# Cross-attention matrices of seven batches made in the first batch's walk, kept in DRAM and loaded per batch

## The reference, cut to what matters

```python
q = einsum('bqm,mhd->bqhd', layernorm(x), Wq) + bq      # bq is not zero here
k = einsum('bkm,mhd->bkhd', ctx, Wk) + bk
v = einsum('bkm,mhd->bkhd', ctx, Wv) + bv
attn = softmax(einsum('bqhd,bkhd->bhqk', q / sqrt(64), k))
x = x + einsum('bqhd,hdm->bqm', einsum('bhqk,bkhd->bqhd', attn, v), Wo) + bo
```

## Time and profile before

| | us |
|---|---|
| three runs | 1469.76, 1473.22 (median), 1481.17 |
| the profiled execution | 1470.44 |
| its span, first to last instruction | 1468.6 |
| PE busy | 1324.8 (90%) |
| DVE busy | 835.2 (57%) |
| POOL busy | 688.1 (47%) |
| ACT busy | 611.2 (42%) |

### The profile page before, as it was taken

How to read it: one execution, slowest core, us unless ns; L and a number is a source line. 1 busy time by engine, 2 the same in 40 slices (tenths; PEclk the granted TensorE clock), 3 DMA queues, 4 the chain that set the end, 5 groups by cost and what they waited for, 6 DMA issues and landing times.

```text
span 1468.6 us, 22253 instructions
## 1 busy us (share of the span) xinstructions
PE 1324.8 (90%) x6717; PEld 841.1 (57%) x6718; DVE 835.2 (57%) x2358; ACT 611.2 (42%) x1278; POOL 688.1 (47%) x1113
## 2 busy tenths in 40 slices
PE   6886899899989998998899889988989789999995
PEld 5542456556655665566556655665566246666663
DVE  2627654864595369436853775386548623333348
ACT  2231554155415531643265236424541544444456
POOL 4312353454445353635354545444544445555557
PEclk9998899999999999999999999999999899999998
DMA  6053204110501050105000500240032534422255
GB/s 215 1 164 127 84 1 122 52 31 1 144 30 31 1 155 19 30 8 162 20 15 29 144 17 15 65 108 17 1 108 66 157 111 129 129 86 86 86 201 175
DMA packets 78300, 115.38 MB, mean 79 GB/s; under 512 B 24840, under 2 KB 66208, under 8 KB 75648
## 3 DMA queue, kind: packets, MB, share of 16 engines
q1 hardware_dynamic: 67888, 79.69, 18.2%
q10 hardware_dynamic: 3840, 16.78, 4.3%
q0 software_dynamic: 6480, 17.77, 3.4%
HBM read 70.22 MB, written 43.59 MB: 77 GB/s over the span
## 4 chain that ended last, share of the span: by engine, by line
PE 59%; DVE 21%; ACT 7%; issue 4%; POOL 4%; ACTq 2%; DMA 2%; SPq 0%; POOLq 0%; DVEq 0%
PE ps L1097 9%; DVE ps L1559 8%; PE ps L930 7%; PE ps L911 6%; PE ps L1019 5%; PE ps L1006 4%; PE ps L1114 4%; PE ps L1061 4%; PE ps L980 3%; PE ps L945 2%; ACTq L1230 2%; PE ps L1071 2%; ACT room L1239 2%; PE ps L1041 2%; PE ps L881 2%
## 5 line engine op out<-in xcount | busy, mean ns | idle before, releaser
L1559 DVE CUSTOM_DVE_ANT_0 ps<-ps,mask_wide 128x128 f32<-128x128 f32 (+3 forms) x512 | 236.9, 522 | 43.6 <-PE ps L980 43.4
L1239 ACT ACTIVATE room<-ps 128x512 f32<-128x512 f32 x320 | 179.8, 599 | 151.4 <-PE ps L1006 151.1
L1061 PE MATMUL ps<-hT,w 128*128 128x512 f32 x768 | 204.5, 410 | 0.0
L706 POOL TENSOR_SCALAR_AFFINE_SELECT room<-room 128x256 f32<-128x256 f32 (+1 forms) x320 | 120.9, 388 | 136.9 <-ACT room L1239 132.2
L1061 PEld LDWEIGHTS ps<-hT,w 128*128 128x128 f32 x768 | 140.4, 188 | 31.4 <-DVE hT L1591 2.0
L980 PE MATMUL ps<-room 96*128 96x128 bf16 (+3 forms) x512 | 110.5, 311 | 51.9 <-DVE nm L1559 38.9
L1071 PE MATMUL ps<-w,room 128*128 128x256 f32 x512 | 132.4, 388 | 15.2 <-POOL room L758 15.0
L758 POOL TENSOR_TENSOR room<-room 128x512 f32<-128x512 f32 x64 | 85.5, 1336 | 117.1 <-DVE room L1603 85.9
L1097 PE MATMUL ps<-room 128*128 x284 | 135.4, 599 | 1.9 <-ACT room L1299 1.9
L930 PE MATMUL ps<-room 128*128 128x256 f32 x512 | 123.2, 385 | 2.8 <-ACT room L1200 1.8
L911 PE MATMUL ps<-room,xnT 128*128 128x512 f32 x256 | 122.0, 601 | 0.0
(11 more groups left out here) (234 smaller groups left out, 2370.1 us busy)
## 6 DMA issues: line engine op xcount, KB each, us to landing
room<-parts_d SPq DMA_DIRECT2D x48, 256.0 KB, 9.0
room<-parts_d ACTq DMA_DIRECT2D x48, 256.0 KB, 6.6
room<-xs_d SPq DMA_DIRECT2D x71, 129.0 KB, 2.1
parts_d<-room SPq DMA_DIRECT2D x64, 128.0 KB, 1.8
room<-pair_d SPq DMA_DIRECT2D x8, 1024.0 KB, 8.2
room<-in_L_ffn_ew SPq DMA_DIRECT2D x24, 256.0 KB, 5.3
xin<-in_x SPq DMA_DIRECT2D x8, 512.0 KB, 11.4
parts_d<-xnT SPq DMA_DIRECT2D x32, 128.0 KB, 1.8
```

What stands on the lines that cost most here:

```text
L706: done(g.affine_select(out=w, in_=w, compare_op=ALU.is_ge, fill=0.0, base=0, pattern=[[0, 2]] * (blocks - 1) + [[1, P]], channel_multiplie ...
L1061: last = mm(bank(up_banks(b, m)[i]), w[:, x, k, m * P:(m + 1) * P], hT[:, y, k, :], start=((x, y, k) == terms[0]), stop=((x, y, k) == term ...
L1239: done(fn(prob[:, u * 512:(u + 1) * 512], bank(score_bank(b) + n % 2), ACT.Exp), "b_exp")
L1559: last = v.tensor_tensor_reduce(bank(nmax % 2 * 2 + i, n), bank(nmax % 2 * 2 + i, n), mask_wide[:, S - n:S], 1.0, LOWEST, ALU.add, ALU.max ...
```

## The change

`m`, `bqk` and `vw` leave the step list of walks 1 to 7. In walk 0 they stay for batch 0, and the 16 `kv` steps become 48 `early` steps. For each pair of heads: `kv` (keys and values, two PSUM banks), `mh` twice (the two halves of M for batches 1 to 7), `bh` (bqk), `vh` twice (VW). In `mh`, `bh` and `vh` the two heads of a pair lie in partitions 0 to 63 and 64 to 127 and are multiplied as two row tiles of PE, each with a contraction of 64 and its own bank, with no block-diagonal zeros. ACT and DVE copy one bank each in the first 30 early steps, ACT both in the rest. ACT issues the stores: per pair one for M (7 batches x 128 x 1 KB), two for bqk, four for VW (64 x 4 x 1 KB each). The staging tiles lie in the room of w1 and w3.

Per batch SP now issues `load_m` (1 MB, and a 4 KB row spread to 128 partitions) once the previous walk's four `sc_add` are done, and `load_vw` (1 MB) ahead of `send_shifts(c, 1)`. `bq_bc` is no longer made per batch. `interleaved()` spreads the scores from `x_turn` 1 on, over 23 slots where there were 28 from `bqk` 0 on, so `sum` 0 and `x_bias` now stand ahead of score unit 7 of group 0, where they stood behind unit 11's (counting on into group 1). The list of walks 1 to 7 up to `ct` 0 becomes: x_turn 0, x_turn 1, sc 0, sc 1, shift 1, f_hb, cs 00, sc 2, sc 3, cs 01, sc 4, sc 5, sc 6, exp 0, sum 0, x_bias, cs 10, va 0 0, sc 7, cs 11, sc 8, sc 9, ct 00, va 0 1.

```diff
 PER = dict(
+    m_in=32, vw_in=16, m_ps=10, m_act=8, m_dve=2, ...
+ONCE = ("kv_in", "bq", "m_ps", "m_act", "m_dve")
+NOT_FIRST = ("y", "y_out", "m_in", "vw_in")
-CROSS = [
+CROSS_FIRST = [
...
+CROSS = [s for s in CROSS_FIRST if s[0] not in ("m", "bqk", "vw")]
-    first, last = CROSS.index(("bqk", 0)), CROSS.index(("ct", 3, 1))
+    first, last = CROSS.index(("x_turn", 1)), CROSS.index(("ct", 3, 1))
+EARLY = [("kv", 0), ("kv", 1)]
+for _a in range(PAIRS):
+    EARLY += [("mh", _a, 0), ("mh", _a, 1), ("bh", _a), ("vh", _a, 0), ("vh", _a, 1)] + ([("kv", _a + 2)] if _a + 2 < PAIRS else [])
+SHARED = 30
 def first_walk():
...
+        crossed += s[0] in ON_PE
+        at_max = s[0] == "max" and (s[1] * T + s[2]) % 3 != 2
+        count = {"v": 2, "route": 3, "slots": 4}.get(s[0], 1 if at_max or s[0] in ON_PE and crossed % 4 == 0 else 0)
+        order += [("early", i) for i in range(n, min(n + count, len(EARLY)))]
 # SP
+            def load_m(b):
+                done(sp.dma_start(m_in, m_d[b, :, :, :, :]), "m_in", 16)
+                done(sp.dma_start(bqk_in, bqk_d[b, :].partition_broadcast(P)), "m_in", 16)
+            def load_vw(b):
+                done(sp.dma_start(vw, vw_d[b, :, :, :]), "vw_in", 16)
                 if c is not None:
+                    if b is not None:
+                        before(sp, c, "y")
+                        load_vw(b)
                     send_shifts(c, 1)
-                        load_kv(b + 1)
+                        need(sp, b, "sc_add", T)
+                        load_m(b + 1)
                     if c is None:
-                        for i in range(4):
-                            sp.wait_ge(kv_out[i], 16 * 2 * PAIRS // 4)
+                        early_landed()
                         sp.sem_inc(freed, 1)
-                        load_kv(b + 1)
+                        load_m(b + 1)
 # PE
+                    if kind == "early":
+                        lo, hi = (4, 5) if n % 2 == 0 else (6, 7)
+                        if n >= 2:
+                            pe.wait_ge(pre["act"], n - 1)
+                            pe.wait_ge(pre["dve"], min(n - 1, SHARED))
...
+                            for c2 in range(2 if what == "vh" else 1):
+                                for i, to in enumerate((lo, hi)):
+                                    rows = slice(i * CHD, (i + 1) * CHD)
+                                    if what == "mh":
+                                        last = mm(bank(to, (B - 1) * CK), wqT[rows, a, k * P:(k + 1) * P], kT[a % 2][rows, CK:], ...)
+                                    elif what == "bh":
+                                        last = mm(bank(to, (B - 1) * CK)[0:1, :], bq[rows, a:a + 1], kT[a % 2][rows, CK:], ...)
+                                    else:
+                                        last = mm(bank(to, D, c2 * D), vT[a % 2][rows, at:at + P], wo_c[rows, a, :], ...)
                     elif kind == "x_turn":
+                        if c is not None and step[1] == 0:
+                            need(pe, c, "a_max", per["a_max"] - 1)
 # ACT
+            def store_early(n):
+                act.wait_ge(pre["act"], n + 1)
+                act.wait_ge(pre["dve"], min(n + 1, SHARED))
+                if what == "mh":
+                    act.dma_start(m_d[1:B, :, a, :, :].rearrange("b p k n -> p b (k n)"), m_st[a % 2]...)
...
+                    if kind == "early":
+                        act.wait_ge(pre["ps"], n + 1)
+                        if EARLY[n][-1] == 0 and what == "mh" and a >= 2:
+                            act.wait_ge(pre[f"m_out{a % 2}"], 16 * (a // 2))
+                        if what == "bh" and a >= 1:
+                            act.wait_ge(pre["bqk_out"], 16 * 2 * a)
+                        for i, src in enumerate((lo, hi)[0:1 if n < SHARED else 2]):
...
+                        if n:
+                            store_early(n - 1)
                     elif kind == "w_split":
+                        store_early(len(EARLY) - 1)
+                        (waits for every store)
 # DVE
                     elif kind == "cs" and step[2]:
+                        elif t == 0:
+                            need(dve, c, "m_in", 32)
+                            need(dve, c, "scat", per["scat"])
+                            if c == 0:
+                                dve.wait_ge(p0["split"], 2)
```

More of the change, by code:

```diff
@@ L145, in first_walk @@
         order.append(s)
[L146 to L151, removed]
+        crossed += s[0] in ON_PE
+        at_max = s[0] == "max" and (s[1] * T + s[2]) % 3 != 2
+        count = {"v": 2, "route": 3, "slots": 4}.get(s[0], 1 if at_max or s[0] in ON_PE and crossed % 4 == 0 else 0)
+        order += [("early", i) for i in range(n, min(n + count, len(EARLY)))]
+        n = min(n + count, len(EARLY))
+    assert n == len(EARLY), n
     return order + [("w_split",)]
@@ L240, in xattn_ffn @@
         wo = sb("wo", [P, KD, D])
+        with nc.sbuf_tensor("early", [P, 4 * KD * FF], F32) as early:
+            pass
         w1 = sb("w1", [P, 2, KD, FF], F32R)
@@ L338, in xattn_ffn @@
         av = sb("av", [P, 512])
+        bqk_st = [t.rearrange("p (b n) -> p b n", n=CK) for t in (early[0:1, 7680:7680 + (B - 1) * CK], av[0:1, 0:(B - 1) * CK])]
         st1 = sb("st1", [P, T, 6])
@@ L709, in batch @@
                         if c == 0:
-                            for i in range(2):
-                                pool.wait_ge(kv_out[i], 16 * 2 * PAIRS // 4)
+                            pool.wait_ge(pre["ps"], len(EARLY))
                         need(pool, c, "xn2", T)
@@ L876, in batch @@
                             need(pe, b, "kv_in", 64)
-                        if c is not None and half == 0:
-                            need(pe, c, "a_max", per["a_max"] - 1 + k)
                         for a in range(4):
@@ L910, in batch @@
                         for k in range(KD):
-                            last = mm(bank(half), xnT[:, k, t * P:(t + 1) * P], m_sb[:, k, half * 512:(half + 1) * 512], start=(k == 0), stop=(k == KD - 1))
+                            last = mm(bank(half), xnT[:, k, t * P:(t + 1) * P], m_sb[:, k, half * 512:(half + 1) * 512] if c is None else m_in[:, half * 4:half * 4 + 4, k, :], start=(k == 0), stop=(k == KD - 1))
                         if half:
@@ L1459, in batch @@
                         s3 = s_sb[:, t % 2, :].rearrange("p (h k) -> p h k", h=CH)
-                        done(v.tensor_tensor(s_sb[:, t % 2, :], ps[:, 0:1024], bqk, ALU.add), "sc_add")
+                        done(v.tensor_tensor(s_sb[:, t % 2, :], ps[:, 0:1024], bqk if c is None else bqk_in, ALU.add), "sc_add")
                         need(dve, b, "sc_add", t + 1)
```

204 lines of the change are left out of this document (130 added, 74 removed).

## The result

The changed kernel takes **1550.62 us** (1547.11 to 1552.59, four runs) where the kernel before takes 1472.46 on the same chip: a ratio of **1.051, interval [1.047, 1.056]**. The forecast was 1496, with 1525 as the end of its range. The direction was right, the size was not: +78 us where I had about +26.

What follows compares the result with a forecast made beforehand. PE looked full in the walks, but new waits of 7.8 us would offset 9.25 removed; DMA and hand-overs bound walk 0. Walk 0 and the step to walk 1 +38, six walks -12, on 1470.4: 1496, range 1452 to 1525.

Steps and rivals of the forecast that it cites:

- What waits instead: Walk 2: PE idles 2.8 us before `sc` 0, 0.6 around `cs` 10, 2.0 before `ct` 00, 2.4 before `va` 0 1.
- Walk 1's own part: Up to the scaling of walk 1: +1.5 us, the new waits eating what walk 1 saves.
- Walk 0 up to the maxima: Walk 0: +13 us to the first `wq` matmul, +10 (0 to 25) from there to the first maximum.
- PE's row tiles: Walk 0's `mh`, `bh`, `vh`: full overlap of two row tiles, 32 us more PE work, 64 as the other end.
- The change of tiling: Around walk 0's early steps: switching PE's tiling costs nothing, since an earlier row showed no gap.
- ACT's issues: Walk 0: 56 DMA issues on ACT at 0.33 us or more each.
- The maxima and the step to walk 1: Walk 0's maxima +6 us (0 to 18); `cs` 00 of walk 1 comes 18 us after the maxima, before 10.5.
- The loads: Per-walk loads of M and vw are hidden and cost nothing; 1 MB takes about 8.2 us, 1.5 MB 12.
- Rival 1: PE stays the bound: walks save 6.5 us each, walk 0 costs 20, total 1451 (1430 with all 9.25 saved); chance 0.18.
- Rival 2: Stores or unpaired row tiles jam walk 0, which then costs 55 to 65 us: 1520; chance 0.14.
- Rival 3: Walk 0 absorbs most of it (+18 us), walks save 2 to 4, total 1473, no change; chance 0.18.
- sign of being wrong: Prediction is wrong if the walks shorten by over 5 us or walk 0 grows by less than 20.

Runs made afterwards that it cites:

- the thinned kernel: Kernel before, order kept, with part of the `m`, `bqk` and `vw` matmuls of walks 1 to 7 left out: 1471.63 us, 0.998.
- the last combination: Changed kernel with `x_bias` and score units later, packed stores, w1 and w3 loaded earlier, no early steps behind the routing: 1498.06 us, 1.018 of the kernel before.
- tripled turns: Changed kernel with each `x_turn` transpose of walks 1 to 7 done three times over: 1535.94 us, 1.041 of the kernel before.
- w1 and w3 first: Changed kernel with SP loading w1 and w3 ahead of its wait for the last stores and M's loads: 1544.10 us, 1.047 of the kernel before.
- small loads: Changed kernel with walks 1 to 7 loading only one pair's block of M and vw: 1548.74 us, 1.052 of the kernel before.
- Narrow products: Changed kernel with walk 0's `mh`, `bh` and `vh` multiplying one block of 64 columns: 1551.95 us, 1.054 of the kernel before.

## Why the prediction was right and wrong

**What waits instead: right.** Four waits were named, with 7.8 us; the four groups of PE show 8.1 more. That PE's work would not turn into time was the core of the forecast, and the thinned kernel shows it in the old order too.

**The clock: the step that failed.** "The new idle time is 7.8 us against 9.25 removed" took the rest of PE's work at full clock, a term put at nothing without a word. Behind each of the two long waits of walk 2 the clock was 0.50, and busy time fell by 4.0 us per walk in all. With idle time 8.2 up, that makes +4.2 per walk where I had -2. The 6.2 us between them are: 4.1 of busy time lost with the clock (3.2 of them in the four groups), by the row of the last combination; 1.1 by which 9.25 was too much, since the same row has 8.2; and 0.9 of idle time, where I had credited 0.5 of the old and none was given back. Over six walks this is 37 of the 56 us of difference between the two profiled executions and my sum of +26. Two of the tripled turns' rows (clock 1.00, `cs` back at 61.6) show the clock as cause and not as a by-product.

**Walk 1's own part** has the same waits ahead of `ct` 00 and `va` 0 1 (1.61 and 3.00 us) and `cs` 00 at half clock (3.75 us, behind a wait of 14.6 for `xnT`): +6.0 where I had +1.5.

**Walk 0 up to the maxima: sizes off.** 17.2 and 16.7 where I had 13 and 10. The reading that DMA bounds walk 0 was wrong: with one seventh of the stores it took 5 us less at most.
- PE's row tiles: forecast 32 us with full overlap. The changed kernel's groups:

```profile
L906 PE MATMUL ps<-room,o_tok 64*128 64x256 f32 x128 | 20.0, 447 | 0.1
L901 PE MATMUL ps<-hb,room 64*128 64x448 f32 x64 | 16.2, 587 | 0.0
L903 PE MATMUL ps<-hb,bq 64*1 64x448 f32 x32 | 7.9, 572 | 7.3 <-ACT early L1244 7.3
```

  Together 44.1 us, a part of it at half clock. In PE's timeline four passes of a pair start 0.95 us before the next instruction (106.28 to 107.23), against 1.5 one after another: a gain of 1.6 and not 2. The estimate of 42 us from the Trainium skill's page "TensorE: Matmul & The Clock Gate" (Part 3) was nearer than my 32.
- The change of tiling: forecast nothing, because the earlier trace rows showed no gap. It costs something, though little. Full-array passes of 264 columns start 0.22 us apart; the last two ahead of the row tiles take 0.54 us, 0.10 more than two of them:

```profile
105.74 0.61 PE L998 MATMUL ps<-wv,xn2T 128*128 128x264 f32 x2
106.28 0.65 PE L901 MATMUL ps<-hb,room 64*128 64x448 f32 x2
```

  The trace has 0.09 to 0.10 us at every change where PE does not wait, in both directions, and also in the earlier trace rows's place: the last 256-column pass of `vw` starts 0.31 us ahead of `va`, where 0.22 lies between two passes. Two changes for each of 40 early steps would be some 7 us of PE at most, an estimate. The Trainium skill ("TensorEngine Tiling (Array Packing)", Key Properties) says that such a change drains the engine. The trace agrees that a change costs time, 0.09 us or so each; whether that is a drain or a weight load that is not covered, no run here tells.
- ACT's issues: forecast 0.33 each. `vw` cost 3.24 to 4.11 us for four, `bqk` 0.77 each. From 96.7 to 151.7 ACT's issues add up to 22.0 us, six loads of `parts_d` among them, where the kernel before has 7.3 in the same part (ten stores of 0.33 to 0.35 and the six loads in 4.00). This was a mis-sized term. Taken away, it gave back some 5 us ahead of the first `wq` matmul, and 1.4 on the way, which is within the spread.
- What does set the 16.7 us is only partly settled. About half goes when products, copies and stores are all small; the other half stays with the steps, their hand-overs and the lower clock, which no run parts. No single one of the costs gives back more than 5 on the way. That the next one then takes its place was not shown; that a lighter PE loses clock was. Which hand-over a shorter walk 0 would need is open.

**The maxima and the step to walk 1: right** (+5.2 for 6, 18.1 for 18), and the second was undone by w1 and w3 first, for the reason that the forecast gave.

**The loads: right.** Within the walks, small loads changed nothing.

**The rivals.** Rival 1 (PE stays the bound) is refuted by the waits, and by the thinned kernel. Rival 2 named the right place and a part of the size (walk 0 at +46.5 with the step to walk 1), by the wrong mechanism: the row tiles paired and the DMA was not jammed. Rival 3 had walk 0 at +18 and the walks shorter; neither came. Not one of them, and neither sign of being wrong, had the walks become slower, so the range ended 25 us too low.

## What to carry to other kernels

Before taking work off an engine that is 99% busy, look for the other engine that ends at the same moment. Thinning the work in place, order kept, asks that in one run. Where the new order leaves PE idle as long as here (2.66 and 3.00 us), price some of the work behind the gap at half clock as well as the gap, and check first whether one line of another engine's order (here POOL's `x_bias`) causes it. And a DMA's issue time on the engine that copies is part of that engine's load: read it in its queue's rows, which the busy time leaves out.

## What the runs showed of the hardware

- **Less work, slower engine.** Gaps of 2.66 and 3.00 us in walk 2 were each followed by a stretch at 0.50. Narrow products took the maxima's clock from 0.98 to 0.64 and their time from 43.2 to 48.5 us, the row below; tripled turns took 9 us of walk 2 from 0.64 to 1.00.

```profile
149.30:197.80 48.50, 39.80 (x178) 18.35 (x176) 33.52 (x142) 18.79 (x37) 11.51 (x11) 0.64 0.64 186
```

- **The cost of an issue depends on the DMA's shape.** On ACT, four stores of `vw` with 1 KB pieces (256 KB each) took 3.24 to 4.11 us to issue, one packed store of the same megabyte 0.34, one of `m` (896 KB) 0.38.
- **Two row tiles** of four f32 passes of 448 columns (two for each tile) take 0.95 us in place of 1.5, at full clock.
- **A change of tiling mode** costs 0.09 us between passes that do not wait: 0.31 us from a 256-column pass to the next start, where it is 0.22 without a change.
